# Two unused buffers ahead of the weights and ahead of the data of a two-layer graph attention kernel

## The chip, the cores and the metric

One core of a Trainium2 chip runs the kernel. The metric is the device time of one launch, in microseconds (us), the median of several launches. In one partition of its on-chip memory (SBUF) every buffer lies at an address in bytes; this text speaks of such addresses modulo 512.

## The reference

The input is 128 graphs of 128 nodes with 256 features, and one 128 x 128 adjacency matrix for each. Two layers follow each other. Cut to what matters:

```python
# layer A, 8 heads of 32, 4 hops
q, k, v = x @ Wq.T + bq, x @ Wk.T + bk, x @ Wv.T + bv
pros = softmax(where(adj == 0, -16384, q_h @ k_h.T))
z = v
for _ in range(4):
    z = 0.9 * (pros @ z) + 0.1 * v
x = layernorm(x + z) * gamma + beta
# layer B, 8 heads of 32
nx = layernorm(x) * ln1_g + ln1_b
attn = softmax((nx @ wq + bq) @ (nx @ wk + bk).T / sqrt(32) + bias(adj))
x1 = x + (attn @ (nx @ wv + bv)) @ wo + bo
n2 = layernorm(x1) * ln2_g + ln2_b
out = x1 + gelu(n2 @ w1 + b1) @ w2 + b2        # 256 -> 1024 -> 256
```

## The kernel before

The graphs are worked on in 64 pairs. One pair goes through 84 steps; the table ORDER names them and says by how many rounds each lags, so that steps of up to six pairs stand between each other, and every engine walks through the same list and carries out what is its own. Nothing in this change touches the list, and nothing in it depends on addresses.

TensorE does four kinds of work.

- **Dense products** (`by_parts`, line 288, and `down`, line 405). A float32 product is made from three faster ones: each operand is split into a high and a low part of type float32r, and high x high, high x low and low x high are added up. Each of the three is a load of 128 x 128 stationary values (LDWEIGHTS) and a matmul with 256 moving columns. In `project` (the steps qA, kA, qB, kB) and `up` (u0 to u3) the split weights are stationary and the data (`inT_A`, `inT_B`, `inT_C`) moves; in `values` (vA, vB), `output` (o) and `down` (d0, d1) the data (`inT`, `oT`, `hT`) is stationary and the split weights move. A pair has 48 products in `project`, 24 in `values`, 12 in `output`, 48 in `up` and 48 in `down`: 180.
- **Transposes** (`turn`, `turn_probs`, `turn_back`, lines 298, 343 and 371): 128 x 128 each, with the data stationary and the unit matrix `ident` moving. A pair has 8 + 32 + 16 = 56.
- **Scores** (line 334): products of 32 rows, `qT` stationary and `kT` moving, four at a time in four row groups of the array. Two instructions each.
- **Hops and attention** (`mix`, line 351): 32 stationary columns, `probsT` moving, four at a time in four column groups. Two instructions each.

In the rows of the profile the moving operand stands first: `ring_ps<-inT_C_high,w_high` moves `inT_C_high` over the stationary `w1_high`.

Buffers are given out one behind the other in the order of the calls of `sb`, each start rounded up to a multiple of 32 bytes, from byte 16,512 of each partition on. `parts` makes two buffers, `_high` and `_low`. So the order in the code sets the addresses, and these follow from the sizes:

| buffers | address modulo 512, before |
|---|---|
| split weights (`wA`, `wB`, `wo`, `w1`, `w2`), all sizes multiples of 2048 bytes | 128 |
| small columns | 128 to 384 |
| rows (`bvA_row` to `b2_row`), `ident`, `ones`, `h1_wide` | 416 |
| `x_sb`, `xT_sb`, `adj`, masks, `inT`, `qT`, `kT`, `v`, `xv`, `z`, `y`, `x1`, `probs`, `probsT`, `zT`, `oT`, `x1b`, `nx`, `n2`, `x2`, `hidden`, `hT` | 0 |

Every slice that a dense product reads begins a multiple of 512 bytes behind the start of its buffer: a stationary slice is 128 values (512 bytes), a moving one 256 values (1024 bytes). So in every dense product one operand begins at 128 and the other at 0.

Of the kernel before, what the change touches and what calls it, by code (L numbers as in the profile page):

```python
# [13 lines left out]
P = 128  # L14
# [83 lines left out]
def build(nc, x, xT, adj, WqT, bq, WkT, bk, WvT, bv, gamma, beta, ln1_g, ln1_b, ln2_g, ln2_b,  # L98
# [10 lines left out]
    with ExitStack() as ctx:  # L109
        def sb(name, shape, dt=F32):  # L110
            return ctx.enter_context(nc.sbuf_tensor(name, shape, dt))
# [4 lines left out]
        def parts(name, shape):  # L116
            return sb(name + "_high", shape, F32R), sb(name + "_low", shape, F32R)

        wA = {n: parts(f"wA_{n}", [P, C, H]) for n in "qkv"}
        wB = {n: parts(f"wB_{n}", [P, C, H]) for n in "qkv"}  # L120
        wo_p = parts("wo", [P, C, H])
# [13 lines left out]
        h1_wide = sb("h1_wide", [P, C, P])  # L135
        tenth, eps, minus_half = sb("tenth", [P, 1]), sb("eps", [P, 1]), sb("minus_half", [P, 1])

        x_sb = sb("x_sb", [P, GB, H])
        xT_sb = sb("xT_sb", [P, C, T])
        adj_sb = {l: sb(f"adj_{l}", [P, GB, P], I32) for l in "AB"}  # L140
# [604 lines left out]
```

## Time and profile before

| | |
|---|---|
| median of three runs | 2363.1 us (2363.02 to 2365.95) |
| the profiled execution's own time | 2364.01 us |
| its span, first to last instruction | 2362.2 us |
| TensorE matmul busy | 2282.8 us, 97% of the span, 29,492 matmuls |
| ScalarE busy | 1919.9 us, 81% |
| VectorE busy | 1745.2 us, 74% |
| GpSimd busy | 1510.8 us, 64% |
| mean granted TensorE clock | 0.996 of full |

Busy time of TensorE is from the start of a matmul to its modelled end, and a matmul starts before the last one has ended, so 97% says only that it has hardly any gaps. How fast it goes is read from the distance between the starts of neighbouring matmuls, which the timeline view gives. The mean ns of a group is the time of one instruction from start to end, which is two to three times that distance.

### The profile page before, as it was taken

To read this page: it belongs to the slowest core of one execution; us is meant where nothing else is said; L and a number is where in the kernel's file an instruction comes from. 1 tells how busy PE (TensorE), PEld (TensorE's weight loads), DVE (VectorE), ACT (ScalarE), POOL (GpSimd) and SP (SyncE) were. 2 spreads that over 40 slices of the span, in tenths; PEclk is the share of its full clock that TensorE was granted. 3 is DMA by queue.
4 is the path that set the end of the run, shared out by engine and by line. 5 is a ranking of instruction groups with operands and counts; after the bars stand their busy time and mean duration, and the time that the engine had idled before them with its cause. 6 is when DMAs were issued, how large, how long until landed. Compare 5 with 4: busy or idle time off the path is not lost.

```text
span 2362.2 us, 77819 instructions
## 1 busy us (share of the span) xinstructions
PE 2282.8 (97%) x29492; PEld 2175.0 (92%) x29492; DVE 1745.2 (74%) x7009; ACT 1919.9 (81%) x6462; POOL 1510.8 (64%) x1610
## 2 busy tenths in 40 slices
PE   2799999999999999999999999999999999999987
PEld 2689999999999999999999999999999999999987
DVE  2578778777777777777777877877877877877863
ACT  0678888888888888888888888888888888888874
POOL 0676666666666666666666666666666666666652
PEclk9999999999999999999999999999999999999999
DMA  3110110110110111011011011011011011011000
GB/s 96 35 33 24 33 38 25 33 38 25 33 38 26 31 38 31 27 38 31 27 38 37 20 37 38 20 38 37 20 37 38 20 37 38 22 35 38 20 15 15
DMA packets 95729, 76.85 MB, mean 33 GB/s; under 512 B 9600, under 2 KB 95104, under 8 KB 95360
## 3 DMA queue, kind: packets, MB, share of 16 engines
q1 hardware_dynamic: 95360, 71.87, 9.9%
q8 instruction: 239, 3.92, 0.7%
q14 instruction: 130, 1.06, 0.2%
HBM read 55.06 MB, written 16.78 MB: 30 GB/s over the span
## 4 chain that ended last, share of the span: by engine, by line
PE 93%; ACT 3%; DVE 1%; issue 1%; POOL 0%; DMA 0%; ACTq 0%; DVEq 0%; POOLq 0%
PE ring_ps L288 41%; PE ring_ps L405 15%; PE ring_ps L351 13%; PE ring_ps L343 10%; PE score_ps L334 6%; PE ring_ps L371 5%; PE ring_ps L298 3%; ACT probs L439 1%; ACT hidden L467 0%; ACT hT_high L467 0%; DVE w_low L504 0%; POOL probs L681 0%; DVE probs L539 0%; ACT zT L453 0%; ACT L467 0%
## 5 line engine op out<-in xcount | busy, mean ns | idle before, releaser
L439 ACT ACTIVATE probs<-probs,negmax 128x128 f32<-128x128 f32 x2048 | 796.4, 396 | 11.6 <-DVE negmax L539 4.5
L681 POOL TENSOR_TENSOR probs<-probs,rinv 128x512 f32<-128x512 f32 x512 | 533.0, 1062 | 113.3 <-DVE rinv L553 113.3
L439 ACT ACTIVATION_READ_ACCUMULATOR probs<-probs,negmax 128x1 f32 x2048 | 399.8, 195 | 0.0
L453 ACT ACTIVATE zT<-ring_ps 128x512 f32<-128x512 f32 x256 | 158.1, 618 | 213.4 <-PE ring_ps L351 213.4
L288 PE MATMUL ring_ps<-inT_C_high,w_high 128*128 128x256 f32 x1024 | 305.5, 298 | 1.5 <-DVE inT_C_low L520 1.4
L343 PE MATMUL ring_ps<-ident,probs 128*128 128x128 f32 x2048 | 295.0, 277 | 6.2 <-POOL probs L681 4.4
L405 PE MATMUL ring_ps<-w_high,hT_high 128*128 128x256 f32 x1024 | 299.1, 292 | 1.8 <-ACT hT_high L467 1.5
L288 PE MATMUL ring_ps<-inT_C_high,w_low 128*128 128x256 f32 x1024 | 289.6, 283 | 0.0
L288 PE MATMUL ring_ps<-inT_C_low,w_high 128*128 128x256 f32 x1024 | 289.4, 283 | 0.0
L405 PE MATMUL ring_ps<-w_high,hT_low 128*128 128x256 f32 x1024 | 288.1, 281 | 0.0
L405 PE MATMUL ring_ps<-w_low,hT_high 128*128 128x256 f32 x1024 | 287.1, 280 | 0.0
L612 DVE TENSOR_TENSOR hT_low<-hidden,hT_high 128x512 fp32r<-128x512 f32 x256 | 226.2, 883 | 64.7 <-ACT hT_high L467 60.6
L343 PEld LDWEIGHTS ring_ps<-ident,probs 128*128 128x128 f32 x2048 | 229.1, 141 | 32.7 <-issue 27.2
L539 DVE CUSTOM_DVE_ANT_0 probs<-score_ps,mask_B 128x128 f32<-128x128 f32 x1024 | 228.7, 284 | 30.4 <-PE score_ps L334 30.4
L687 POOL TENSOR_TENSOR rstd<-moments,eps 128x2 f32<-128x2 f32 x192 | 37.7, 196 | 327.6 <-DVE moments L599 327.6
L539 DVE CUSTOM_DVE_ANT_0 probs<-score_ps,mask_A 128x128 f32<-128x128 f32 x1024 | 229.6, 285 | 8.2 <-issue 7.7
L467 ACT ACTIVATE hidden<-ring_ps,b_col 128x256 f32<-128x256 f32 x512 | 219.4, 492 | 15.3 <-PE ring_ps L288 14.6
L585 DVE TENSOR_TENSOR x<-ring_ps,x1b 128x512 f32<-128x512 f32 x64 | 44.3, 692 | 244.4 <-PE ring_ps L288 242.6
L467 ACT ACTIVATE hT_high<-ring_ps,b_col 128x256 fp32r<-128x256 f32 x512 | 221.4, 505 | 0.0
L351 PE MATMUL ring_ps<-probsT_A,z 128*32 128x128 f32 x6144 | 207.5, 276 | 7.2 <-DVE z L566 7.2
L288 PEld LDWEIGHTS ring_ps<-inT_C_high,w_high 128*128 128x128 f32 x1024 | 194.6, 190 | 2.1 <-DVE inT_C_low L520 1.8
L405 PEld LDWEIGHTS ring_ps<-w_high,hT_high 128*128 128x128 f32 x1024 | 192.8, 188 | 2.7 <-ACT hT_high L467 2.0
(148 smaller groups left out, 7377.1 us busy)
## 6 DMA issues: line engine op xcount, KB each, us to landing
xT_sb<-in_xT_dram SPq DMA_DIRECT2D x64, 256.0 KB, 3.1
x_sb<-in_x_dram SPq DMA_DIRECT2D x64, 256.0 KB, 2.8
out_dram<-x SPq DMA_DIRECT2D x128, 128.0 KB, 2.0
adj_A<-in_adj_dram SPq DMA_DIRECT2D x64, 128.0 KB, 3.1
adj_B<-in_adj_dram SPq DMA_DIRECT2D x64, 128.0 KB, 2.3
probsT_A<-in_L_gnn_w_dram SPq DMA_DIRECT2D x1, 1024.0 KB, 7.5
probsT_B<-in_L_gnn_w_dram SPq DMA_DIRECT2D x1, 1024.0 KB, 9.2
probs<-in_L_gnn_Wq_dram SPq DMA_DIRECT2D x1, 256.0 KB, 2.9
```

Source lines behind the costliest of these rows:

```text
L288: mm = pe.matmul(dst, left(a, kc), right(b, kc), start=(n == 0), stop=(n == len(pairs) - 1))
L334: mm = pe.matmul(score_ps[:, r, (b * C + c) * P:(b * C + c + 1) * P], qT[l][r * HD:(r + 1) * HD, c, b * P:(b + 1) * P], kT[l][r * HD:(r + ...
L343: mm = pe.transpose(ring(name, g)[:, r * P:(r + 1) * P], probs[:, UNIT[l, b], half * HR + r, :], ident[:, :])
L351: mm = pe.matmul(ring(name, g)[r * HD:(r + 1) * HD, (b * C + c) * P:(b * C + c + 1) * P], src[:, b, h * HD:(h + 1) * HD], prT[:, b, h, :], ...
L371: mm = pe.transpose(ring(name, g)[:, at:at + P], zT[k][:, b, c, :], ident[:, :])
L405: mm = pe.matmul(ring(name, g)[:, 0:H], hT[a][:, f, b * P:(b + 1) * P], w2_p[c][:, f, :], start=(n == 0), stop=(n == len(pairs) - 1))
L439: e = act.activation(probs[:, u, h, :], probs[:, u, h, :], ACT.Exp, bias=negmax[:, u, h:h + 1], scale=-1.0, accum_out=sums[:, u, h:h + 1])
L453: act.activation(zT[k][:, :, :, :], ring(name, g).rearrange("p (b c n) -> p b c n", b=GB, c=C), ACT.Copy).then_inc(s_out[name], 1)
L467: e = act.activation(dst[:, i, :], ring(name, g)[:, i * T:(i + 1) * T], ACT.Gelu, bias=b1_col[:, 2 * f + i:2 * f + i + 1])
L539: t = dve.tensor_tensor_reduce(probs[:, u, h, :], score_ps[:, r, (b * C + half) * P:(b * C + half + 1) * P], mask[l][:, b, :], -1.0, HIGHE ...
L612: dve.tensor_tensor(hT[1][:, 2 * f:2 * f + 2, :], hidden[:, f % 2, :, :], hT[0][:, 2 * f:2 * f + 2, :], ALU.subtract).then_inc(s_h_low[nam ...
L681: pool.tensor_tensor(probs[:, u, hs, :], probs[:, u, hs, :], rinv[:, u, hs].unsqueeze(2).to_broadcast([P, HR, P]), ALU.mult).then_inc(s_pr ...
```

## The change

It allocates a buffer `apart` of 32 float32 values a partition (128 bytes) ahead of the weights, and a buffer `apart_too` of 96 values (384 bytes) ahead of `x_sb`. Nothing reads or writes them.

```diff
         def parts(name, shape):
             return sb(name + "_high", shape, F32R), sb(name + "_low", shape, F32R)
 
+
+        sb("apart", [P, 32])
         wA = {n: parts(f"wA_{n}", [P, C, H]) for n in "qkv"}
         wB = {n: parts(f"wB_{n}", [P, C, H]) for n in "qkv"}
...
         tenth, eps, minus_half = sb("tenth", [P, 1]), sb("eps", [P, 1]), sb("minus_half", [P, 1])
 
+        sb("apart_too", [P, 96])
         x_sb = sb("x_sb", [P, GB, H])
```

All instructions of all five engines stay the same and in the same order; only addresses in them change. Modulo 512 the split weights go from 128 to 256, the small columns move up by 128, the rows, `ident`, `ones` and `h1_wide` go from 416 to 32, and everything from `x_sb` on stays at 0 (it lies 512 bytes higher). In every dense product one operand now begins at 256 and the other at 0. In every transpose the moving `ident` begins at 32 where it began at 416, and the stationary data at 0 as before. Scores and hops keep their places.

## Rows read from the trace of the kernel before

**Rows 1.** The page: span, busy time, granted clock by slices, and the chain that ended last.
```profile
span 2362.2 us, 77819 instructions
PE 2282.8 (97%) x29492; PEld 2175.0 (92%) x29492; DVE 1745.2 (74%) x7009; ACT 1919.9 (81%) x6462; POOL 1510.8 (64%) x1610
...
PEclk9999999999999999999999999999999999999999
...
PE 93%; ACT 3%; DVE 1%; issue 1%; POOL 0%; DMA 0%; ACTq 0%; DVEq 0%; POOLq 0%
```
**Rows 2.** Busy time by stretches, two stretches of 600 us each.
```profile
600.00:1200.00 600.00, 600.00 (x7833) 573.39 (x7832) 460.92 (x1862) 511.64 (x1723) 402.39 (x426) 1.00 0.10 32
1200.00:1800.00 600.00, 600.00 (x7833) 573.39 (x7832) 460.90 (x1865) 511.64 (x1723) 402.42 (x428) 1.00 0.11 32
```
**Rows 3.** TensorE's groups of the whole span, by form: count, busy us, mean ns.
```profile
L288 PE MATMUL ring_ps<-inT_C_low,w_high 128*128 128x256 f32 x1024 | 289.4, 283 | 0.0
L405 PE MATMUL ring_ps<-w_high,hT_low 128*128 128x256 f32 x1024 | 288.1, 281 | 0.0
L288 PE MATMUL ring_ps<-inT_B_low,wB_k_high 128*128 128x256 f32 x256 | 72.9, 285 | 0.0
L288 PE MATMUL ring_ps<-wo_low,oT_high 128*128 128x256 f32 x256 | 71.3, 279 | 0.0
L343 PE MATMUL ring_ps<-ident,probs 128*128 128x128 f32 x2048 | 295.0, 277 | 6.2 <-POOL probs L681 4.4 <-ACT hT_high L467 1.7
L371 PE MATMUL ring_ps<-ident,zT 128*128 128x128 f32 x1024 | 157.4, 276 | 2.0 <-ACT zT L453 1.8
L298 PE MATMUL ring_ps<-ident,nx 128*128 128x128 f32 x256 | 42.0, 286 | 0.4 <-DVE nx L606 0.4
```
**Rows 4.** Timeline of TensorE, first of kB's twelve products to the transpose behind: start us, us.
```profile
802.77 0.28 PE L288 MATMUL ring_ps<-inT_B_high,wB_k_high 128*128 128x256 f32 x1
...
804.21 0.38 PE L343 MATMUL ring_ps<-ident,probs 128*128 128x128 f32 x2
```
**Rows 5.** The same view, steps kA and o, their second and last products.
```profile
703.23 0.28 PE L288 MATMUL ring_ps<-inT_A_low,wA_k_high 128*128 128x256 f32 x1
...
704.40 0.28 PE L288 MATMUL ring_ps<-inT_A_high,wA_k_low 128*128 128x256 f32 x1
...
839.99 0.28 PE L288 MATMUL ring_ps<-wo_low,oT_high 128*128 128x256 f32 x1
...
841.17 0.28 PE L288 MATMUL ring_ps<-wo_high,oT_low 128*128 128x256 f32 x1
```
**Rows 6.** The same view: eight transposes (pA10, pA11), and twenty matmuls of scores.
```profile
739.74 1.04 PE L343 MATMUL ring_ps<-ident,probs 128*128 128x128 f32 x8
...
715.31 0.74 PE L334 MATMUL score_ps<-kT_A,qT_A 32*128 32x128 f32 x20
```
**Rows 7.** A stretch at the lower clock: busy by stretch (third figure from the end: clock).
```profile
66.00:72.60 6.60, 5.48 (x25) 5.20 (x26) 1.64 (x10) 4.04 (x19) 5.36 (x6) 0.50 0.26 79
```
**Rows 8.** Timeline of TensorE in that stretch, two of the twelve products of a kA.
```profile
69.25 0.42 PE L288 MATMUL ring_ps<-inT_A_low,wA_k_high 128*128 128x256 f32 x1
...
71.38 0.41 PE L288 MATMUL ring_ps<-inT_A_high,wA_k_low 128*128 128x256 f32 x1
```
**Rows 9.** Timeline of TensorE and its weight loads where step u2 gives way to sA.
```profile
714.76 0.28 PE L288 MATMUL ring_ps<-inT_C_low,w_high 128*128 128x256 f32 x1
714.77 0.19 PEld L288 LDWEIGHTS ring_ps<-inT_C_high,w_low 128*128 128x128 f32 x1
714.88 0.28 PE L288 MATMUL ring_ps<-inT_C_high,w_low 128*128 128x256 f32 x1
715.09 0.31 PEld L334 LDWEIGHTS score_ps<-kT_A,qT_A 32*128 32x128 f32 x8
```
**Rows 10.** Groups by form, 714.87 to 715.00 us (products of rows 9), and 715.60 to 715.75 us.
```profile
L288 PE MATMUL ring_ps<-inT_C_low,w_high 128*128 128x256 f32 x1 | 0.3, 280 | 0.0
L288 PE MATMUL ring_ps<-inT_C_high,w_low 128*128 128x256 f32 x1 | 0.3, 280 | 0.0
...
L334 PE MATMUL score_ps<-kT_A,qT_A 32*128 32x128 f32 x12 | 0.5, 270 | 0.0
```

## The prediction

> **What bounds the kernel now.** I read four views in this order. The page first: the chain that ended last is TensorE for 93% of the span, and the clock is granted in full in all slices [rows 1]. The stretches next: in 600 us out of the middle TensorE is busy for all 600 us, ScalarE for 512 us (85%), VectorE and GpSimd for less [rows 2]. So in the steady part nothing makes TensorE wait, and the time is the sum of the distances between the starts of its matmuls. The groups then say what the matmuls are: 11,520 dense products of 256 columns (180 a pair; the groups of `inT_C`, `hT` and the seven smaller weights have 1024 and 256 records a form) and 2048 + 1024 + 512 = 3,584 transposes [rows 3]. Last the timeline, for the distances:
>
> - kB: twelve products from 802.77 to 804.21, 120 ns each [rows 4]. kA and o: ten distances in 1.18 us each, 118 ns [rows 5]. Over all dense steps I take 119 ns, since the mean duration moves with the distance (279 ns in o, 285 ns in kB) and the large groups show 281 to 283 ns [rows 3].
> - Transposes: eight in 1.04 us, of which one lasts 0.27, so (1.04 - 0.27)/7 = 110 ns. Scores, five groups of four in 0.74 us: (0.74 - 0.27 - 0.02)/4 = 0.112 us for each four [rows 6].
>
> A dense product takes about 9 to 10 ns more than a transpose, and that excess is all the change can be after. At the lower granted clock, 0.50 of full, that is 1.2 GHz [rows 7], the ten distances take 2.13 us, 213 ns each [rows 8]. That is 256 columns at 1.2 GHz to the nanosecond; at 2.4 GHz 256 columns would take 107 ns, and the trace shows 118 to 120. So the excess is there only at the full clock.
>
> **The change part by part.** No instruction is added, removed or moved, no semaphore, no transfer changes, and the two buffers cost no time. What is left is three places where addresses could set a time.
>
> (a) Dense products, 11,520. One operand goes from 128 to 256 modulo 512, the other stays at 0. The question is whether the weight load of the next product, which starts 10 ns after a product does [rows 9], gets in the way of its moving columns, and whether their distance matters. Three rows speak:
> 1. At 714.88 stands the last product of u2. The next weight load starts only 0.21 us later, at 715.09, so this product streams its columns with no load beside it [rows 9]. It takes 280 ns. The product ahead of it, with a load beside it, takes 280 ns too; a matmul of scores takes 270 [rows 10]. The excess of 10 ns is there with no second reader. It belongs to 256 columns at the full clock, not to a meeting of two reads.
> 2. The roles are turned round between kA (weights at 128 stationary, data at 0 moving) and o (the other way), and both go at 118 ns [rows 5]. A read that runs ahead by 128 and one that runs behind by 128 cost the same.
> 3. kB has the same addresses modulo 512 as kA and is 2 ns slower [rows 4, 5]. So something other than these addresses sets the small differences.
>
> I take 0. The bounds: downwards, what a load beside a product costs, 282 ns for the groups against 280 for the one alone [rows 3, 10], 2 ns x 11,520 = 23 us; and at the very far end the whole excess over a transpose, 10 ns x 11,520 = 115 us. Upwards: every dense product goes in kB's rhythm, 1 ns x 11,520 = 12 us.
>
> The Trainium skill ("TensorE: Matmul & The Clock Gate", Part 2, "Step-by-step: what each phase is for") says that TensorE has two independent SBUF read ports and that loading the next weights takes nothing from the running matmul. By that rule (a) is 0 whatever the addresses, and the product that ran alone agrees at 280 ns. The same page (Part 2, "Back-to-back issue gap") gives N/2.4 + 2.5 ns for a warm stream, 109 ns at 256 columns. By that rule the 119 ns hold 10 ns that need not be there, and the sum would be -115 us if the move freed them.
>
> (b) Transposes, 3,584. The moving `ident` goes from 416 to 32 while the stationary data stays at 0. In scores both operands begin at 0 and four matmuls take 112 ns against the transposes' 110 [rows 6], so a near meeting could cost 2 to 3 ns. I take 0, since scores use row groups and two instructions, which transposes don't; bounds 0 and 3 ns x 3,584 = +11 us. A gain has no room: 110 ns is the shortest distance of a full load and matmul here.
>
> (c) VectorE, ScalarE and GpSimd read the small columns and rows at new places. They are covered by TensorE: ScalarE has 88 us of 600 to spare [rows 2], so an operation would have to get over 15% longer to show. 0.
>
> Sum: 0. The profiled execution took 2364.01 us with a span of 2362.2; the median of the three runs is 2363.1, 0.9 us less. The forecast is the median, **2363.1 us**. A measurement of this kernel can tell about 0.2% from no change, 4.7 us, which is only 0.41 ns for each dense product. So "no change" asks for a great deal of indifference.
>
> **The rivals.**
>
> Faster: the two reads do meet, somewhere in each product, and half a period apart (256) is where they meet least. For it: kA and kB differ by 2 ns with the same addresses, so the distance is not fixed by the count of columns alone, and some give and take between load and product is possible. Against it: the three points under (a). Price: near end 2 ns x 11,520 = 23 us, 2340 us; far end by the gap of a transpose, 115 us, 2248 us. What comes off arrives almost whole, since even at the far end ScalarE's 512 us would fill only 90% of a stretch that shrinks from 600 to 571 us [rows 2]. It decides from 0.41 ns a product.
>
> Slower: `ident` at 32 comes close under the data at 0, and each transpose loses what scores show. 3 ns x 3,584 = 11 us, 2374 us. For it: the 112 against 110 ns. Against it: scores are another kind of instruction, and their 2 ns may be their own. It decides from 1.3 ns a transpose (4.7 us / 3,584). A second way to the same side: the shift puts all dense steps into kB's rhythm, +12 us, 2375 us.
>
> That the change doesn't do what it says is not open: the addresses follow from the sizes, 16,512 + 128 = 16,640, which is 256 modulo 512, and 86,656 + 384 = 87,040, which is 0.
>
> **How the numbers follow.** No effect: 0.47. Faster: 0.36, of which 0.25 near 23 us and up to 40, and 0.11 beyond. Slower: 0.17, `ident` 0.10 and the rhythm 0.07. The likeliest is no effect, so 2363.1. The range reaches down to 2322, which leaves out the far end of the faster case (0.11), and up to 2380, above both slower prices, leaving out some 0.03. The likeliest case's own range is 2358 to 2368.
>
> **What would show it.** If right: the products of `inT_C`, `hT` and kB keep 281 to 285 ns, kB keeps 120 ns a product, the transposes 110 ns, and the product alone 280. If the faster case holds, kB and kA fall together below 117 ns and the product alone stays at 280, or falls too, which would say that the excess was in its own read after all. If the slower one, eight transposes last over 1.05 us with the dense groups unmoved. The forecast is wrong if the dense distances move by over 0.4 ns in either direction.

## The result

The changed kernel takes 2372.34 us (median of 7 runs, 2371.22 to 2373.20) against 2364.10 us before (7 runs, 2363.02 to 2365.95). The ratio is 1.0034, with a 95% interval of 1.0022 to 1.0046: slower by 0.34%, 8.2 us, clear of the 0.2% that can be told. The forecast was no change. The time lies inside the range that was given (2322 to 2380), on the side that had a chance of 0.17.

The page of the changed kernel, its span and busy times, against [rows 1] (line numbers in its rows are three higher than before):

```profile
span 2370.8 us, 77819 instructions
PE 2291.6 (97%) x29492; PEld 2183.4 (92%) x29492; DVE 1696.5 (72%) x7009; ACT 1919.8 (81%) x6462; POOL 1511.8 (64%) x1610
```

The span grew by 8.6 us, and so did TensorE's busy time, by 8.8. The number of matmuls is the same. The stretches say the same as [rows 2] with one difference:

```profile
600.00:1200.00 600.00, 600.00 (x7808) 573.58 (x7811) 445.01 (x1848) 510.32 (x1717) 401.08 (x426) 1.00 0.11 32
1200.00:1800.00 600.00, 600.00 (x7809) 573.50 (x7800) 445.38 (x1851) 510.37 (x1717) 401.30 (x425) 1.00 0.10 32
```

TensorE is still busy for all 600 us at the full clock, but it gets through 7808 matmuls where it got through 7833, 0.32% fewer. It waits for nobody; it has become slower. VectorE lost 49 us of busy time. One operation lost 52 us (`edges<-adj_B`, a mean of 1231 ns before and 417 ns now), and another took 7 us more (`hT_low`). TensorE stayed busy throughout, so that bought nothing. It is 417 ns as well in the two other kernels below whose products go at 120 ns (weights alone moved, weights at 0), with `ident` back at 416; why was not looked into.

The groups of the whole span, the same as in [rows 3]:

```profile
L346 PE MATMUL ring_ps<-ident,probs 128*128 128x128 f32 x2048 | 293.9, 276 | 6.5 <-POOL probs L684 4.8 <-ACT hT_high L470 1.7
L291 PE MATMUL ring_ps<-inT_C_low,w_high 128*128 128x256 f32 x1024 | 290.5, 284 | 0.0
L408 PE MATMUL ring_ps<-w_high,hT_low 128*128 128x256 f32 x1024 | 288.9, 282 | 0.0
L291 PE MATMUL ring_ps<-inT_B_low,wB_k_high 128*128 128x256 f32 x256 | 72.9, 285 | 0.0
L291 PE MATMUL ring_ps<-wo_low,oT_high 128*128 128x256 f32 x256 | 72.3, 283 | 0.0
```

The transposes are unmoved. `wo_low,oT_high` went from 279 to 283 ns, `inT_C` and `hT` each up by 1, and `wB_k` stands still at 285. The timeline shows what that is: the second and last products of kA, the first of kB with the transpose behind it, and the second and last of o, in the same pair as in [rows 4, 5], and the eight transposes of [rows 6]:

```profile
706.43 0.28 PE L291 MATMUL ring_ps<-inT_A_low,wA_k_high 128*128 128x256 f32 x1
...
707.63 0.28 PE L291 MATMUL ring_ps<-inT_A_high,wA_k_low 128*128 128x256 f32 x1
...
743.08 1.04 PE L346 MATMUL ring_ps<-ident,probs 128*128 128x128 f32 x8
...
806.30 0.28 PE L291 MATMUL ring_ps<-inT_B_high,wB_k_high 128*128 128x256 f32 x1
...
807.74 0.27 PE L346 MATMUL ring_ps<-ident,probs 128*128 128x128 f32 x1
...
843.63 0.28 PE L291 MATMUL ring_ps<-wo_low,oT_high 128*128 128x256 f32 x1
...
844.83 0.28 PE L291 MATMUL ring_ps<-wo_high,oT_low 128*128 128x256 f32 x1
```

kB takes 1.44 us for twelve, as before. kA and o now take 1.20 us for ten distances where they took 1.18: they have gone from 118 to kB's 120 ns. Eight transposes still last 1.04 us.

The records of single matmuls in pairs 5 to 58 tell it finer. The first distance of a step that follows other work is long, 199 to 207 ns, and is left out here and in all means of dense products below; a pair has 156 distances without it. Their mean was 118.67 ns and is 119.44 ns. Before, ten of the thirteen steps ran in a lasting cycle of five distances, 115, 118, 122, 120, 119 ns, and the other three (qB, kB, u0) in a cycle of 119 and 121. Now, after some uneven products at the start, every step settles at 120.0. The change is 156 x 0.77 ns x 64 pairs = 7.7 us, which is nearly all of the 8.2.

### The profile page after: what moved, and what is told of

It is laid out like the page before. It is cut to its first block, busy times and chain, and to the rows that moved or that the text cites. A ratio compares the mean times of both kernels' runs of the same rounds, so it can differ in the third digit from the quotient of the medians.

```text
span 2370.8 us, 77819 instructions
## 1 busy us (share of the span) xinstructions
PE 2291.6 (97%) x29492; PEld 2183.4 (92%) x29492; DVE 1696.5 (72%) x7009; ACT 1919.8 (81%) x6462; POOL 1511.8 (64%) x1610
## 4 chain that ended last, share of the span: by engine, by line
PE 93%; ACT 3%; DVE 1%; issue 1%; POOL 0%; DMA 0%; ACTq 0%; DVEq 0%; POOLq 0%
PE ring_ps L291 41%; PE ring_ps L408 15%; PE ring_ps L354 13%; PE ring_ps L346 10%; PE score_ps L337 6%; PE ring_ps L374 5%; PE ring_ps L301 3%; ACT probs L442 1%; ACT hidden L470 0%; ACT hT_high L470 0%; POOL probs L684 0%; DVE w_low L507 0%; DVE probs L542 0%; ACT zT L456 0%; ACT L470 0%
## 5 line engine op out<-in xcount | busy, mean ns | idle before, releaser
L684 POOL TENSOR_TENSOR probs<-probs,rinv 128x512 f32<-128x512 f32 x512 | 539.1, 1073 | 116.1 <-DVE rinv L556 116.0
L615 DVE TENSOR_TENSOR hT_low<-hidden,hT_high 128x512 fp32r<-128x512 f32 x256 | 233.4, 912 | 113.4 <-ACT hT_high L470 113.3
```

What stands on the lines that cost most here:

```text
L615: dve.tensor_tensor(hT[1][:, 2 * f:2 * f + 2, :], hidden[:, f % 2, :, :], hT[0][:, 2 * f:2 * f + 2, :], ALU.subtract).then_inc(s_h_low[nam ...
L684: pool.tensor_tensor(probs[:, u, hs, :], probs[:, u, hs, :], rinv[:, u, hs].unsqueeze(2).to_broadcast([P, HR, P]), ALU.mult).then_inc(s_pr ...
```

## The experiments

Fourteen kernels ran, all with the computation unchanged and only unused buffers (or the order of the weight buffers) different. Each was compared with the kernel before on the same chip. The distance in a dense product means the start address of one operand less the start address of the other. For all of them I give the time and the ratio to before with its interval, and for most the mean distance in time between dense products inside a step, as above. The time from one pair to the next, where it is given, is the mean over pairs 5 to 58; its difference to before, times 64 pairs, follows the measured times in all sixteen kernels.

**Weights or `ident`?** The change moves both. First kernel: the weights alone.

```diff
+        sb("pad_a", [P, 32])
         wA = {n: parts(f"wA_{n}", [P, C, H]) for n in "qkv"}
...
+        sb("pad_m", [P, 96])
         colA = {n: sb(f"colA_{n}", [P, C]) for n in "qk"}
```

> Weights at 256, data at 0, ident back at 416 (its place before). Theory D (the distance of the two operands of a dense product sets its rhythm): all of the loss stays, 2372 us, dense products settle at 120 ns each, transposes at 109 ns. Rival I (ident at 32 costs the time): back to 2364 us. Rival S (chance: any shift of the layout changes the rhythm a little): some other time, 2360 to 2376 us.

Second kernel: `ident` alone (with the 512 bytes higher addresses of everything from `x_sb` on).

```diff
+        sb("pad_m", [P, 32])
         colA = {n: sb(f"colA_{n}", [P, C]) for n in "qk"}
...
+        sb("pad_b", [P, 96])
         x_sb = sb("x_sb", [P, GB, H])
```

> Weights at 128 and data at 0 as before, ident at 32 as in the change, and everything from x_sb on 512 bytes higher as in the change. Theory D: 2364 us, dense products keep the rhythm of five (112 to 123 ns, mean 118.8). Rival I: 2372 us. Rival S: anything between 2360 and 2376 us.

Measured: the weights alone give 2374.73 us, 1.0035 (1.0022 to 1.0049), 119.33 ns. `ident` alone gives 2366.46 us, 1.0002 (0.9994 to 1.0011), 118.70 ns. The whole loss comes with the weights. (With the weights alone the 156 distances make 6.6 us of it, and the first distances, a mean of 203.7 ns against 202.4 before, make another 1.0.) `ident` changes how the steps begin and which uneven distances they run through, but hardly their mean.

**Which distance?** Two more positions of the weights, with `ident` at 416 and the data at 0. Weights at 0:

```diff
+        sb("pad_a", [P, 96])
         wA = {n: parts(f"wA_{n}", [P, C, H]) for n in "qkv"}
...
+        sb("pad_m", [P, 32])
         colA = {n: sb(f"colA_{n}", [P, C]) for n in "qk"}
```

> Weights and data both at 0, ident at 416. Theory D with a period of 256: distance 0 is the same as 256, so 2372 us and 120 ns a product. Theory D with a period of 512: its own rhythm, neither 118.8 nor necessarily 120 ns; if the two reads collide when they lie over each other, it is slower than 2372 us, by up to 10 ns x 11,520 = 115 us. Rival I: 2364 us, as ident has its old place.

Weights at 384:

```diff
+        sb("pad_a", [P, 64])
         wA = {n: parts(f"wA_{n}", [P, C, H]) for n in "qkv"}
...
+        sb("pad_m", [P, 64])
         colA = {n: sb(f"colA_{n}", [P, C]) for n in "qk"}
```

> Weights at 384, data at 0, ident at 416: the distance is 128 the other way round. Theory D: since the two roles of weights and data had the same rhythm before, +128 and -128 are alike, so 2364 us and the rhythm of five. Rival S: 2360 to 2376 us without a rule. Rival I: 2364 us.

Measured: at 0, 2374.03 us, 1.0035 (1.0021 to 1.0048); at 384, 2364.29 us, 0.9998 (0.9989 to 1.0007). The records say more than the times. From one pair to the next it takes 35.3533 us with the weights at 0 and 35.3533 us with the weights at 256 and `ident` at 416; it takes 35.2199 us with the weights at 384 and 35.2199 us before. Place by place in each step, the mean distances agree within 0.04 ns. So 0 and 256 are the same to the kernel, and 128 and 384 are. Addresses modulo 512 were the wrong measure: the period is 256, and the change moved the operands from half a period apart to right over each other.

**The distance or the address?** Only the first buffer, so that everything moves up by 128:

```diff
+        sb("pad_a", [P, 32])
         wA = {n: parts(f"wA_{n}", [P, C, H]) for n in "qkv"}
```

> Only the first buffer: everything moves up by 128, weights at 256, ident at 32, data at 128. All distances are those of before. Theory R (only the distance between operands counts): 2364 us and before's rhythm, 118.7 to 119.1 ns a product. Rival A (the address itself counts, weights at 256 are bad): 2372 us and 120 ns.

Measured: 2364.90 us, 1.0001 (0.9991 to 1.0010), and again 35.2199 us a pair. The weights lie at 256 and `ident` at 32 here as in the changed kernel, and nothing is lost. Only the distances count.

**Other distances.** Weights at 64 (`pad_a` of 112 values, `pad_m` of 16), at 32 (104 and 24), at 96 (120 and 8), all with the data at 0 and `ident` at 416.

> Weights at 64, data at 0, ident at 416. After four runs distances 0 and 256 give the same rhythm step by step, and 128 and 384 too. Theory 256 (the rhythm depends on the distance modulo 256): 64 is a quarter of the period, with a rhythm of its own, between the two or outside them (2355 to 2380 us), and since -64 is not +64 the two roles may part: project and up against values, output and down. Rival 32 (a finer period that 128 is not a multiple of can't be; one of which 128 is an odd multiple of the half): only multiples of 256 are bad, 64 behaves like 128, 2364 us.

> Weights at 32, data at 0, ident at 416. If the two reads must lie exactly over each other to lock at 120 ns, a distance of 32 already frees them: 2364 us. If nearness counts, it is like distance 0: 2373 us. If the roles part: one of project and values as at 0, the other as at 128.

> Weights at 96, data at 0, ident at 416. Close to the 128 of before; if the rhythm follows the distance smoothly 2364 us, if there is a better distance than 128 it may be here or at 64: down to 2350 us. If only exact multiples of 128 share a rhythm, the steps show patterns seen nowhere yet.

Measured:

| weights at | us | ratio to before | all dense | weights stationary | weights moving |
|---|---|---|---|---|---|
| 32 | 2354.76 | 0.9957 (0.9942 to 0.9972) | 117.67 ns | 118.14 | 117.14 |
| 64 | 2341.93 | 0.9901 (0.9884 to 0.9917) | 116.34 ns | 115.01 | 117.80 |
| 96 | 2371.68 | 1.0027 (1.0017 to 1.0038) | 119.27 ns | 118.94 | 119.63 |
| 128 (before) | 2364.10 | 1 | 118.67 ns | 119.01 | 118.29 |

Other distances do more than the change did, and not smoothly: 64 is the best and 96 is nearly as bad as 0. None of the three times lies where it was expected (2355 to 2380, 2364 or 2373, and 2350 to 2364 us). At 64 the roles part, as they could not at 0 and 128, where plus and minus are the same modulo 256. The timeline at 64, steps kA (weights stationary) and o (weights moving), against [rows 5]:

```profile
698.44 0.28 PE L290 MATMUL ring_ps<-inT_A_high,wA_k_high 128*128 128x256 f32 x1
...
699.35 0.28 PE L290 MATMUL ring_ps<-inT_A_high,wA_k_low 128*128 128x256 f32 x1
...
833.50 0.28 PE L290 MATMUL ring_ps<-wo_low,oT_high 128*128 128x256 f32 x1
...
834.68 0.28 PE L290 MATMUL ring_ps<-wo_high,oT_low 128*128 128x256 f32 x1
```

kA: eight distances in 0.91 us, 113 to 114 ns. o: ten in 1.18 us, 118 ns.

**The period again, and the roles.** Weights at 320 (`pad_a` 48, `pad_m` 80 values):

> All weights at 320, data at 0: 256 above the 64 of the earlier run. Period of 256: the same as at 64, 2342 us, project and up at 114 to 116 ns, values and down at 118. Period of 512: a rhythm of its own, and another time.

Measured: 2344.03 us, 0.9911 (0.9894 to 0.9927), and 34.8533 us a pair, as with 64. The period of 256 holds at a third distance.

Then every dense product with the stationary operand 64 above the moving one. Weights that are stationary stay at 64, those that move go to 192:

```diff
-        wA = {n: parts(f"wA_{n}", [P, C, H]) for n in "qkv"}
-        wB = {n: parts(f"wB_{n}", [P, C, H]) for n in "qkv"}
-        wo_p = parts("wo", [P, C, H])
+        sb("pad_a", [P, 112])
+        wA = {n: parts(f"wA_{n}", [P, C, H]) for n in "qk"}
+        wB = {n: parts(f"wB_{n}", [P, C, H]) for n in "qk"}
         w1_p = parts("w1", [P, C, FF])
+        sb("pad_b", [P, 32])
+        wA["v"], wB["v"] = parts("wA_v", [P, C, H]), parts("wB_v", [P, C, H])
+        wo_p = parts("wo", [P, C, H])
         w2_p = parts("w2", [P, FC, H])
+        sb("pad_c", [P, 112])
```

> Stationary weights (q, k, w1) at 64, moving weights (v, wo, w2) at 192, data at 0, ident at 416: in every dense product the stationary operand now lies 64 above the moving one modulo 256. Theory St (the distance that counts is stationary minus moving; +64 gives 113 to 116 ns, -64 gives 118): all steps at 113 to 115 ns, 11,520 x (118.9 - 114) = 56 us less than before, about 2308 us. Rival Ro (project and up are faster at 64 for another reason of theirs, such as w or inT themselves): values, output and down stay at 118 ns and the time stays at 2342 us.

And its mirror, with the two addresses exchanged (`pad_a` 16, `pad_b` 96, `pad_c` 16 values):

> The mirror: stationary weights at 192, moving weights at 64, so the stationary operand lies 64 below the moving one everywhere. Theory St: every step at 117 to 118 ns, 11,520 x 1.1 = 13 us less than before, about 2352 us. Rival Ro (64 and 192 are good places whatever the role): about 2310 us.

Measured: 2335.54 us for the first, 0.9875 (0.9861 to 0.9890), 115.53 ns; 2353.48 us for the mirror, 0.9951 (0.9936 to 0.9966), 117.49 ns. The direction counts, and steps with moving weights gained from it (117.80 to 116.09 ns) as those with stationary weights had (119.01 to 115.01), so it is the distance and not the role. But 2335 is not the 2308 that I expected: of the steps at +64, some went at 113 ns and others at 118, as qB and kB had already done with all weights at 64. And in the mirror, 2353 us as expected, one step, vB, still went at 113. So at a distance of 64, either way, both paces exist.

**What picks the pace?** `ident` moves, in three ways (`pad_c` larger, and a `pad_d` ahead of `x_sb`; here for 32, against the kernel with the stationary operand 64 above everywhere). The small columns, the rows, `ones` and `h1_wide` move with it, and the data lies 512 bytes higher. The operands of the dense products keep their places modulo 256.

```diff
-        sb("pad_c", [P, 112])
+        sb("pad_c", [P, 144])
...
+        sb("pad_d", [P, 96])
         x_sb = sb("x_sb", [P, GB, H])
```

> Stationary operands 64 above the moving ones everywhere, ident at 32 instead of 416. Theory En (at distance +64 there are two lasting rhythms, 113 and 118 ns, and how a step begins behind the transposes chooses; steps that began at 201 ns stayed at 118): moving ident changes how steps begin, so other steps than d0, o, vB, qB, kB are at 118, and the time is between 2308 us (all at 113) and 2352 us (all at 118). Rival Fi (the rhythm at +64 is fixed by what the step reads): the same steps at 118, 2335 us.

> The same with ident at 0, right over the stationary data of the transposes. Theory En: yet another set of steps at 118 ns, 2308 to 2352 us. Rival Fi: 2335 us and the same set. If a near meeting costs a transpose, transposes go from 109 to 112 ns as well, 3 ns x 3,584 = 11 us more.

> The same with ident at 480, 64 above its old place. Theory En: another set of steps at 118 ns, 2308 to 2352 us; this is also a try for a kernel faster than 2335 us. Rival Fi: 2335 us.

| `ident` at | us | ratio to before | all dense | steps at 118 ns throughout |
|---|---|---|---|---|
| 416 | 2335.54 | 0.9875 (0.9861 to 0.9890) | 115.5 ns | qB, kB, vB, o, d0 |
| 0 | 2333.61 | 0.9870 (0.9853 to 0.9886) | 115.6 | qA, qB, kB, o, d0 |
| 480 | 2329.79 | 0.9846 (0.9831 to 0.9860) | 115.2 | qA, vB, o, d0 |
| 32 | 2323.58 | 0.9821 (0.9806 to 0.9835) | 114.4 | qA, o |

The set of slow steps changes with buffers that they don't read: the second explanation, that a step's own buffers fix its pace, has fallen. kB shows it. With `ident` at 416:

```profile
792.88 0.28 PE L292 MATMUL ring_ps<-inT_B_high,wB_k_high 128*128 128x256 f32 x1
...
794.18 0.28 PE L292 MATMUL ring_ps<-inT_B_high,wB_k_low 128*128 128x256 f32 x1
```

With `ident` at 32:

```profile
790.96 0.28 PE L293 MATMUL ring_ps<-inT_B_high,wB_k_high 128*128 128x256 f32 x1
...
792.21 0.28 PE L293 MATMUL ring_ps<-inT_B_high,wB_k_low 128*128 128x256 f32 x1
```

Eleven distances in 1.30 us (118 ns) and in 1.25 us (114 ns), with the same weights, the same data and the same distance. In the records, qB, which kB continues without a break, begins with 201 ns to its second product in the slow kernel and with 207 in the fast one. In these four kernels all steps that begin with 202 ns or more come down to 113 by their sixth distance. Of those that begin with 200 or 201 ns, the ones whose second distance is 117 to 119 stay at 118, and the ones whose second distance is 120 or 122 come down. This holds for +64 only: in the mirror, steps that begin with 204 or 205 ns stay at 118. Every stretch of dense products follows transposes, which move `ident`, and that is a way for `ident` to change how it begins. That the beginning is what picks the pace is read from these records; no kernel changed the beginning and nothing else. The transposes go at 109 ns in all four, also with `ident` right over the data, so the 3 ns a transpose of that expectation do not exist.

The kernel with `ident` at 32 beats both kernels of this study: 2323.58 us, 1.8% below the one before and 2.1% below the changed one. Its TensorE is still busy throughout, with more matmuls in the same 600 us, and ScalarE fills 522 of them:

```profile
600.00:1200.00 600.00, 600.00 (x8025) 573.11 (x8026) 467.49 (x1894) 521.58 (x1755) 411.02 (x434) 1.00 0.11 32
```

## Why the prediction was wrong

**What bounds the kernel** was right. The time is the sum of distances between matmuls on one engine that waits for nothing, and all sixteen kernels bear it out: the distances from pair to pair, times 64, give +7.3 us for the changed kernel, -23.5 for weights at 64 and -44.0 for the best kernel, and the times moved by +8.2, -22.8 and -42.0. It was also right that 0.41 ns a product decides, and that "no change" asks for a great deal.

**Term (a), put at 0, was the step that failed.** I held that the distance between the two operands does nothing, and it made +0.77 ns a product, 7.7 of the 8.2 us. Three points carried the 0.

**Point 1** failed. I took the product at 714.88 for one that streams with no load beside it, and from its 280 ns that the excess of 10 ns belongs to 256 columns at full clock. I looked only at the next load. The load of the product itself stands in the same rows: it starts at 714.77 and lasts 0.19 us, to 714.96, so by the profile it is still going for the first 80 ns of the product [rows 9]. And the runs show that such a last product is not fixed. With the weights at 32, the timeline where o gives way to scores:

```profile
699.54 0.28 PE L290 MATMUL ring_ps<-wo_low,oT_high 128*128 128x256 f32 x1
699.66 0.27 PE L290 MATMUL ring_ps<-wo_high,oT_low 128*128 128x256 f32 x1
699.86 1.17 PE L336 MATMUL score_ps<-kT_B,qT_B 32*128 32x128 f32 x32
```

And the groups of the same kernel from 699.82 to 699.85 us, when only the last product runs:

```profile
L290 PE MATMUL ring_ps<-wo_high,oT_low 128*128 128x256 f32 x1 | 0.3, 274 | 0.0
```

It took 274 ns where the last product of o took 280 before, and u2's last product, the one of point 1, takes 276 in the records with the weights at 64. So up to 6 of the 10 ns go with the layout, as far as the modelled ends can tell. The near bound of 23 us that I drew from that row was too small: 42 us have come off so far.

**Point 2** read the right thing wrongly. kA and o do go at the same 118 ns with their roles exchanged, but I concluded that the distance has no effect. They are alike because +128 and -128 are the same modulo 256, as the kernel with the weights at 384 shows. Two equal readings at one distance say nothing about another distance.

**Point 3** was a true observation and the better clue. kA and kB have the same distance and differ by 2 ns: kA runs in the cycle of five and kB in that of 119 and 121. With `ident` at 32 and the weights still at 128, kB runs in the cycle of five too. I used the 2 ns against the effect of addresses, and they are the other half of it: the distance sets which lasting paces there are, and something else, by the records the start of a step, picks one.

**Ports and gap.** The trace does not agree with the rule of two independent read ports ("TensorE: Matmul & The Clock Gate", Part 2, "Step-by-step: what each phase is for", in the Trainium skill), as far as it would make the place of the operands free: with the instructions the same, buffer addresses make 2.1% between the best and the changed kernel. What stands between a load and a moving read is not shown. The 109 ns worked out from the same page's "Back-to-back issue gap" in the Trainium skill, an estimate, were not reached; 113.3 ns is the lowest lasting pace seen. That section also says that the formula is for a matmul taken by itself and that loads change the spacing in a stream, so it was a weak yardstick for these products. Of the 10 ns between 119 and 109, over half can be freed, but not by this move.

**Term (b)**, the transposes: 0, right; they keep 109 ns. **Term (c)**: right. VectorE's times did change, and TensorE did not wait for it.

**The rivals.** The mechanism that happened was priced as the second way to the slower side: all dense steps in kB's rhythm, +12 us, 2375 us. The price is near by luck: from a mean of 118.67 and not 119, a full 120 in every product would have cost 1.33 ns x 11,520 = 15 us. It measured +8.2 us, since the first products of a step still run through some shorter distances, so that the mean is 119.44. It had 0.07 of the chance. The faster rival was wrong for this change (half of 512 is a whole period) and right in kind.

## What to carry to other kernels

Where a matmul engine runs without gaps, read the distance between starts inside each step and not its busy share, and try the start address of one operand against the other in steps of 32 bytes: it costs a few unused bytes, and here the time moved between +0.3% and -1.8% (the latter with the weights reordered and `ident` moved as well). A layout can win or lose this by accident when a buffer that lies between the two operands changes its size; moving both together changed nothing. Before an argument rests on "this one ran alone", look at everything that overlaps it, its own load too. A reading that is the same at two places proves independence only if the two places are different under every period that could be at work.

## What was not expected of the hardware

- The pace of products of 256 float32r columns with a load of 128 x 128 each depends on stationary minus moving start modulo 256 bytes. Lasting paces at full clock: 120.0 ns at distance 0; at 128 a cycle of five with a mean of 118.7 ns, or cycles with a mean of 120 (119 and 121 in turn); 113.3 or 117.8 ns at 64 either way.
- Layouts that differ by 256 (0 and 256; 64 and 320; 128 and 384) gave the same time from pair to pair to 0.1 ns (35.3533, 34.8533, 35.2199 us), in separate launches.
- At the same distance two paces exist. Which one a step takes goes with its first two distances, within some nanoseconds, and it keeps for as long as the step lasts, 24 products in d0 and d1.
- At the lower granted clock, 0.50 of full or 1.2 GHz, there was no excess at all, 213 ns for 256 columns [rows 7, 8].

Open: why 64 is good and 96 is bad, what in the memory repeats every 256 bytes, whether the step that stayed at 118 ns in all four kernels with +64 everywhere (o) can be moved, and whether a product with no load anywhere near it would go at 107 ns. None of this was tried.
